# Block-diagonal attention matmuls in two row tiles of 64 partitions, with scores and values in two shared PSUM banks

## The reference, cut to what matters

```python
Q = (x @ Wq.T).reshape(b, length, 16, 16).swapaxes(-2, -1)     # x after a layer norm; K, V alike from the context
qk = jnp.einsum('blih,bljh->blij', Q, K) / sqrt(16)            # per token: a 16 x 16 matrix over its own features
attn = jax.nn.softmax(qk, axis=-1)
valued = jnp.einsum('blij,bljh->blih', attn, V)
x = x + tanh(g0) * (valued.swapaxes(-2, -1).reshape(b, length, d) @ Wo.T)
# then x + tanh(g1) * the output of the one expert with the largest gate, of the layer norm of x
```

## Time and profile before

| | us |
|---|---|
| median of three runs | 320.98 |
| the profiled execution, by its own time | 319.54 |
| span of that execution in the trace | 317.6 |
| TensorE matmuls busy | 285.0 (90%) |
| TensorE weight loads busy | 217.4 (68%) |
| VectorE busy | 230.9 (73%) |
| ScalarE busy | 84.4 (27%) |
| GpSimd busy | 123.2 (39%) |

### The profile page before, as it was taken

The page is one execution under the profiler, slowest core; times in us unless marked ns, Lnnn a source line. Parts: engine busy times, 40 slices in busy tenths (PEclk is TensorE's granted clock), DMA queues, the critical chain, the costliest instruction groups (busy, mean ns, idle before and its releaser), DMA issues.

```text
span 317.6 us, 10049 instructions
## 1 busy us (share of the span) xinstructions
PE 285.0 (90%) x3151; PEld 217.4 (68%) x3152; DVE 230.9 (73%) x810; ACT 84.4 (27%) x219; POOL 123.2 (39%) x125
## 2 busy tenths in 40 slices
PE   2999999999999999999999996687998899999970
PEld 1548677677677676776776775566877888898860
DVE  6576678797798888888877978855789556556550
ACT  1021321311312302303213213122434344444420
POOL 9321121523523523524424334432354444434441
PEclk9999999999999999999999999967999999999995
DMA  8565245475565575574455123166467878777620
GB/s 263 182 171 146 63 143 151 144 207 174 156 210 162 164 207 142 174 210 103 132 159 145 43 78 84 59 189 195 137 177 238 271 213 234 232 218 213 208 80 0
DMA packets 35482, 51.40 MB, mean 162 GB/s; under 512 B 8189, under 2 KB 18558, under 8 KB 35456
## 3 DMA queue, kind: packets, MB, share of 16 engines
q1 hardware_dynamic: 20272, 25.72, 31.2%
q10 hardware_dynamic: 11776, 16.78, 16.7%
q0 software_dynamic: 3408, 8.59, 7.4%
HBM read 32.99 MB, written 10.60 MB: 137 GB/s over the span
## 4 chain that ended last, share of the span: by engine, by line
PE 65%; DVE 13%; DMA 9%; issue 6%; ACT 2%; POOL 1%; ACTq 1%; SPq 1%; DVEq 1%; POOLq 0%
PE ps_qo L400 14%; PE ps_pr L392 13%; PE ps_tr L550 6%; DMA sb_x<-x_in 6%; PE ps_av L564 5%; PE ps_so L418 5%; PE ps_so L550 5%; PE ps_to L564 5%; PE ps_av L438 5%; PE ps_pr L540 2%; PE ps_tr L427 2%; DMA sb_wkv<-wkv_in 1%; PE ps_to L451 1%; DVE sb_om L787 1%; DVE sb_pe_x L763 1%
## 5 line engine op out<-in xcount | busy, mean ns | idle before, releaser
L392 PE MATMUL ps_pr<-sb_wkv,sb_ct 128*128 128x512 f32 x128 | 64.4, 628 | 6.4 <-DMA sb_wkv<-wkv_in 5.9
L278 POOL TENSOR_TENSOR sb_cn<-sb_om,sb_rt 128x512 f32<-128x512 f32 x15 | 19.3, 1285 | 67.6 <-DVE sb_om L787 67.6
L620 ACT ACTIVATE sb_pe_x<-sb_pe_x 128x512 f32<-128x512 f32 x16 | 10.1, 631 | 123.3 <-DVE sb_pe_x L763 123.3
L392 PEld LDWEIGHTS ps_pr<-sb_wkv,sb_ct 128*128 128x128 f32 x128 | 22.6, 194 | 25.8 <-issue 25.6
L1206 POOL DMA_INDIRECT routed_rows<-sb_xs,sb_pos_i x32 | 32.2, 1006 | 20.5 <-DVE sb_pos_i L878 10.5
L400 PE MATMUL ps_qo<-sb_wog,sb_ot 128*128 128x264 f32 x128 | 34.7, 419 | 1.3 <-ACT sb_q_n L615 1.1
L400 PEld LDWEIGHTS ps_qo<-sb_wog,sb_ot 128*128 128x128 f32 x128 | 26.1, 206 | 11.7 <-issue 7.3
L438 PE MATMUL ps_av<-sb_vb,sb_at 128*32 128x128 f32 x1024 | 31.6, 276 | 0.0
L418 PE MATMUL ps_so<-sb_kb,sb_y_q 128*32 128x128 f32 x1024 | 31.0, 273 | 0.3 <-DMA sb_kb<-sb_y_k 0.3
L400 PE MATMUL ps_qo<-sb_wqg_c,sb_xt 128*128 128x264 f32 x128 | 31.1, 387 | 0.0
L438 PEld LDWEIGHTS ps_av<-sb_vb,sb_at 128*32 128x32 f32 x1024 | 27.2, 111 | 5.6 <-issue 5.5
(11 more groups left out here) (127 smaller groups left out, 488.9 us busy)
## 6 DMA issues: line engine op xcount, KB each, us to landing
sb_w<-w_in_ SPq DMA_DIRECT2D x24, 257.0 KB, 3.1
sb_xb<-routed_rows SPq DMA_DIRECT2D x39, 134.0 KB, 2.5
sb_kb<-sb_y_k SPq DMA_DIRECT2D x125, 32.0 KB
sb_vb<-sb_y_v SPq DMA_DIRECT2D x124, 32.0 KB
sb_w<-w_in_ ACTq DMA_DIRECT2D x15, 257.0 KB, 3.4
sb_ct<-ctx_in ACTq DMA_DIRECT2D x15, 256.0 KB, 3.0
sb_x<-x_in ACTq DMA_DIRECT2D x15, 256.0 KB, 5.3
sb_xt<-xt_in_ ACTq DMA_DIRECT2D x14, 256.0 KB, 3.6
```

The source lines that it names most:

```text
L278: eng.tensor_tensor(cn[:].rearrange("p u h i -> p h u i"), om[:].rearrange("p h (u i) -> p h u i", u=2), rt[:].rearrange("p (u i) -> p u i ...
L392: last = pe.matmul(pr[:, s * 512:(s + 1) * 512], lhsT=ct[i][:, kc, s, :], rhs=wkv[:, kc, :], start=(kc == 0), stop=(kc == KC - 1))
L620: act.activation(pe_x[:], pe_x[:], ACT.Exp, scale=float(H) ** -0.5).then_inc(exp_done, 1)
```

## The change

The same products are formed, but each matmul has 64 partitions instead of 128 and 64 moving columns instead of 128; there are two of them where there was one: half g of the partitions with the four slots that are filled in it. They lie in two row tiles of TensorE's array. Per pair that is 64 matmuls each for scores and values, so 128 MATMUL and 128 LDWEIGHTS instructions each. Half g writes to bank g of a new tensor `sa` of two banks, in which values take columns 0 to 127 and scores columns 128 to 255 of each half bank.

As scores and values now lie in the same two banks, `turn_o(k-1)` on VectorE waits for the scores of k too (`score_done`, n + 2), and the read patterns of `largest`, `shift` and `turn_o` run over both banks. On TensorE the waits of values(k) and of scores(k+1) (K and V landed, `at_out`, `om_done`, `yq_out`, `sub_done`) are moved ahead of `project_o(k-1)`, and scores(k+1) are issued directly behind values(k) in the same slot. Ranks go to `to` instead of `av` (the last two to free parts of other banks), and `vb` keeps its slots in the order of `kb`.

```diff
-        so = ps("so", [P, 512])
-        av = ps("av", [P, 512])
+        sa = ps("sa", [P, 2 * 512])
+        sa_v = sa[:].rearrange("p (g a x) -> p g a x", g=2, a=2)
...
-            def scores(n, i):
-
+            def wait_scores(n, kb_landed):
+                pe.wait_ge(*kb_landed)
                 pe.wait_ge(yq_out, n + 1)
                 wait(pe, sub_done, n)
+
+            def scores(n, i):
                 for r in range(4):
                     for u in range(2):
                         for q in range(4):
                             b = 16 * u + 4 * q + r
-                            last = pe.matmul(so[32 * q:32 * q + 32, r * P:(r + 1) * P],
-                                             lhsT=y_q[:, 4 * q + r, u:u + 2, :].rearrange("p a b -> p (a b)"),
-                                             rhs=kb[i][:, :, H * b:H * b + H], start=(u == 0), stop=(u == 1))
+                            for g in range(2):
+                                half, own = slice(64 * g, 64 * g + 64), slice(4 * g, 4 * g + 4)
+                                last = pe.matmul(sa_v[32 * q:32 * q + 32, g, r // 2, P + 64 * (r % 2):P + 64 * (r % 2) + 64],
+                                                 lhsT=y_q[half, 4 * q + r, u:u + 2, :].rearrange("p a b -> p (a b)"),
+                                                 rhs=kb[i][half, own, H * b:H * b + H], start=(u == 0), stop=(u == 1))
...
             def slot(k, q, t):
-                pe.wait_ge(*landed(kb_in, q, t, 0, SPREAD))
-                scores(k, q)
...
                     project_kv(k + 2, q, 1)
+                if isinstance(k, int) and k == 0:
+                    wo_gates()
+                wait_values(k, landed(vb_in, q, t, 0, SPREAD))
+                if has(k, 1):
+                    wait_scores(k + 1, landed(kb_in, q, t, 1, SPREAD))
                 if has(k, -1):
                     project_o(k - 1)
-                if isinstance(k, int) and k == 0:
-                    wo_gates()
-                pe.wait_ge(*landed(vb_in, q, t, 0, SPREAD))
                 values(k, q)
+                if has(k, 1):
+                    scores(k + 1, 1 - q)
...
             def turn_o(n):
                 wait(dve, cn_done, n)
                 dve.wait_ge(av_done, n + 1)
-                dve.transpose(om[:], av[:].rearrange("p (t h) -> p h t", h=H)).then_inc(om_done, 1)
+                if not isinstance(n, int) or n < last_pair:
+                    dve.wait_ge(score_done, n + 2)
+                dve.transpose(om[:], sa_v[:, :, :, 0:P].rearrange("p g a (t h) -> p h t (g a)", h=H)).then_inc(om_done, 1)
```

More of the change, by code:

```diff
@@ L193, in flamingo_block @@
         x_t_ps = [pr[:, 512 * i:512 * i + D] for i in range(2)]
-        h_ps = [so[:, 0:D], tr[:, 0:D]]
-        y_ps = [av[:, 0:D], to[:, 0:D]]
+        h_ps = [tr[:, 0:D], sa[:, 0:D]]
+        y_ps = [sa[:, 512:512 + D], to[:, 0:D]]
         lap_ps = qo[:, 960:992]
         def rank_ps(n, first, end):
-            bank = qo[:, 448:512] if isinstance(n, int) and n == last_pair else av
+            bank = to
+            if isinstance(n, int) and n == last_pair - 1:
+                bank = sa[:, 512 + D:1024]
+            if isinstance(n, int) and n == last_pair:
+                bank = qo[:, 448:512]
             return bank[:, first:end]
@@ L428, in transpose_a, with wait_values, values @@
                 last.then_inc(at_done, 1)
-            def values(n, i):
+            def wait_values(n, vb_landed):
+                pe.wait_ge(*vb_landed)
                 pe.wait_ge(at_out, n + 1)
                 wait(pe, om_done, n)
-                wait(pe, rank_read, n - 1 if not isinstance(n, int) or n > 1 else 0)
+            def values(n, i):
                 for r in range(4):
@@ L437, in values @@
                             b = 16 * u + 4 * q + r
-                            last = pe.matmul(av[32 * q:32 * q + 32, r * P:(r + 1) * P],
-                                             lhsT=at[:, 4 * r + q, u:u + 2, :].rearrange("p a b -> p (a b)"),
-                                             rhs=vb[i][:, :, H * b:H * b + H], start=(u == 0), stop=(u == 1))
+                            for g in range(2):
+                                half, own = slice(64 * g, 64 * g + 64), slice(4 * g, 4 * g + 4)
+                                last = pe.matmul(sa_v[32 * q:32 * q + 32, g, :, 32 * r:32 * r + 32],
+                                                 lhsT=at[half, 4 * r + q, u:u + 2, :].rearrange("p a b -> p (a b)"),
+                                                 rhs=vb[i][half, own, H * b:H * b + H], start=(u == 0), stop=(u == 1))
                 last.then_inc(av_done, 1)
@@ L445, in transpose_o @@
                 wait(pe, ot_out, n)
+                if not isinstance(n, int) or n < last_pair:
+                    wait(pe, rank_read, n - 1 if not isinstance(n, int) or n > 1 else 0)
                 if isinstance(n, int) and n == 0:
@@ L467, in ranks @@
                 pe.wait_ge(oh_done, n + 1)
-                if not isinstance(n, int) or n < last_pair:
+                if isinstance(n, int) and n == last_pair - 1:
                     pe.wait_ge(om_done, n + 2)
+                elif not isinstance(n, int) or n < last_pair:
+                    pe.wait_ge(ot_out, n + 2)
                 rhs = oh_b[:].rearrange("p s e -> p (s e)")
@@ L528, in pre @@
                 pe.wait_ge(zero_ok, 1)
+                wait_scores(0, (kb_in[0], SPREAD))
+                scores(0, 0)
             slots(pe, pre, slot)
@@ L751, in scores_of, with by_half @@
             def scores_of():
-                return so[:].rearrange("p (t j) -> p t j", j=H)
+                return sa_v[:, :, :, P:2 * P].rearrange("p g a (r t j) -> p g a r t j", r=2, j=H)
+            def by_half(ap):
+                return ap[:].rearrange("p (g a r t) -> p g a r t", g=2, a=2, r=2)
             def largest(n):
                 dve.wait_ge(score_done, n + 1)
-                dve.tensor_reduce(mx[:], scores_of(), AX.X, ALU.max).then_inc(max_done, 1)
+                dve.tensor_reduce(by_half(mx), scores_of(), AX.X, ALU.max).then_inc(max_done, 1)
             def shift(n):
@@ L762, in shift @@
                 dve.wait_ge(max_done, n + 1)
-                dve.tensor_tensor(pe_x[:].rearrange("p (t j) -> p t j", j=H), scores_of(),
-                                  mx[:].unsqueeze(2).broadcast_to([P, 32, H]), ALU.subtract).then_inc(sub_done, 1)
+                dve.tensor_tensor(pe_x[:].rearrange("p (a r g t j) -> p g a r t j", a=2, r=2, g=2, j=H), scores_of(),
+                                  by_half(mx).unsqueeze(5).broadcast_to([P, 2, 2, 2, 4, H]), ALU.subtract).then_inc(sub_done, 1)
             def sums(n):
```

3 lines of the change are left out of this document (1 added, 2 removed).

## The result

The changed kernel takes 388.33 us (median of four runs, 385.97 to 393.69); the kernel before took 321.35 in the same comparison (319.21 to 322.07). The ratio is 1.211, with a 95% interval of 1.205 to 1.218: slower by a fifth. The forecast had the sign and the mechanism, but 337 us is far off and 388 lies above the range of 325 to 380.

What follows compares the result with a forecast made beforehand. TensorE bounds the attention stage, VectorE having only 2.1 us a slot to spare. New stalls make a slot 13.4 us instead of 12.16; 13 slots add 16 us to 319.5, then 1.4 to the median: 337 us, range 325 to 380.

Steps and rivals of the forecast that it cites:

- the constant 11.6: Attention slot's period outside the two matmul phases, in us: 9.57 to `turn_q`'s end, then 0.03, 1.87 and 0.15.
- P: Start-to-start cost of one values or scores matmul phase on TensorE; 1.78 us before the change.
- `turn_o`'s price of 0.71 us: VectorE's `turn_o` reading three strides over two banks: 0.71 us taken, other end +0.3 us a slot.
- The first stall: TensorE waits 1.75 us for the exponential at `transpose_a`; the output's transpose, ready at about +2.3, was taken as covered.
- P = 0.9: All eight tiles run side by side at the first bursts' pace, so each values or scores phase takes 0.9 us.
- R2: Rival: each matmul costs 27.8 ns whatever its columns; phase 3.56 us, slot 18.7 us, 406 us in all; chance 0.10.
- The cost of fetching, 0.3 us a slot: Allowance of 0.3 us a slot for fetching 256 more TensorE instructions per slot, within the range.
- The wait for the indirect DMA, 0.81 us: Wait in VectorE's chain before `turn_q`, taken to move along unchanged at 0.81 us a slot.
- R4: Rival: code fetching or a lower clock in the new stalls, the range's upper part; chance 0.04.
- R1: Rival: row tiles bring nothing; phase 1.78 us, slot 15.2 us, 360 us; chance 0.28 with what lies between.
- the main case: Full tile overlap, phases of 0.9 us, slot 13.4 us, 337 us in all; chance 0.45.
- R3: Rival: VectorE's chain is shorter and TensorE stays the bound; slot 10.4 us, 296 us; chance 0.13 with its neighbours.

Runs made afterwards that it cites:

- The order alone: Kernel before with its old matmuls and banks, but all waits and the scores' place as in the changed kernel: 385.15 us, ratio 1.207.
- the run with 64 columns alone: Kernel before with each scores and values matmul cut into two of 64 columns, all 128 partitions, old banks and order: 331.62 us, ratio 1.043.
- the run with the filler: Changed kernel plus four needless 128 by 264 matmuls in the stall ahead of the output projection: 385.85 us, ratio 1.214.
- The swap of `turn_q` and `place_4`: `turn_q` ahead of `place_4` in VectorE's list: changed kernel 360.28 us, ratio 1.132; kernel before 318.21 us, ratio 0.999.
- the last experiment: Changed kernel with lists reordered by readiness, ranks behind the second K and V projection and `turn_q` ahead of their reading: 348.11 us, ratio 1.090.
- The experiment before it: Changed kernel with lists reordered by readiness: waits back, `turn_q` first, statistics of k-2 ahead of `largest`, `turn_o` behind `shift`: 345.71 us, ratio 1.086.

## Why the prediction was wrong in size, and where it was right

**The bound (right).** TensorE and VectorE were both nearly full, and what VectorE does between the scores and `turn_q` decides. The waits that grew are in that chain; the holes of the first slots are not.

**The mechanism and the constant 11.6 (right, for undisturbed slots).** `turn_o` behind the scores, `transpose_a` late, the output projection behind `turn_q`: each is in the timeline above. The order alone measures 15.3 us a slot where 11.6 + 2P with the P of that kernel gives 15.1 to 15.2; in the changed kernel they take 15.05 where 11.6 and the 3.15 us of its phases make 14.75. `turn_o`'s price of 0.71 us was measured at 0.717. The first stall was split otherwise: a part of it, 0.34 us at 142.95, stands ahead of `transpose_o`, whose division was taken to be covered.

**P = 0.9 (failed).** The step that carried the pace of the first burst through the whole phase was wrong. In the slot shown, values and scores take 3.30 us in place of P + P + 0.15 = 1.95; before the change they took 129.29 - 125.58 = 3.71. So 0.41 us of the 1.76 expected came, about a quarter. The reading of the bursts as such was right, since 32 instructions start in the first 0.25 us, but the pace isn't kept. On four tiles 128 instructions need 1.99 us to their last result and on eight 1.48 at the best, and in the changed kernel's scores 1.9 to 2.0, no better than four. Why the pace falls is open. The Trainium skill speaks on both sides here as well. TensorEngine Tiling (Array Packing), Key Properties, has tiles load weights and multiply in parallel: the trace agrees that they do so in part. TensorE: Matmul & The Clock Gate, "Wait — 56ns, not 53.3ns?", has no two starts closer than about 25 ns: 128 instructions with their last result in 1.48 us are 11.6 ns each (23 ns for an fp32 matmul, which is two of them), so for these small tiles the trace does not agree, and R2 with it falls.

**The cost of fetching, 0.3 us a slot (failed).** The most of it is not spread over the slots. It comes in the first ones, as holes of up to 3.23 us, about 11 us together; the later slots of the run with 64 columns alone are 0.3 us over the mean before. That run has the holes too, without row tiles or a new order. That this is code being loaded is a reading of the instruction queue's packets, of their number and of their place beside the holes; no run held the number of instructions and changed only where the code lies.

**The wait for the indirect DMA, 0.81 us (failed).** It was carried along as a constant, from one row of a wait that nobody waited for. In all it was 10.6 us, 1.7 at the most; with the new order it is:

```profile
DVE sb_pos_i L902 <- DMA routed_rows<-sb_xs,sb_pos_i: 17.4, 11, 3.3
```

The cast's wait grew to 17.4 us, 3.3 at the most, and now all of it stands ahead of `turn_q`. When does it grow? In the longest case SyncE issues a late load of the expert weights 0.36 us behind the second scatter:

```profile
93.61 0.96 POOL L1230 DMA_INDIRECT routed_rows<-sb_xs,sb_pos_i  x1 [0.30 <-issue]
...
93.97 0.48 SPq L331 DMA_DIRECT2D sb_w<-w_in  x1
...
98.89 0.17 DVE L902 CAST sb_pos_i<-sb_pos 128x2 uint32<-128x2 f32 x1 [3.32 <-DMA routed_rows<-sb_xs,sb_pos_i]
```

In the traces of all these kernels every wait of the cast over 2 us, 14 in six kernels, stands where SyncE issues a load of expert weights or biases or a store of padding rows within 1 us of the second scatter; in the four steps of the changed kernel from 188.06 to 248.40, which have none of these DMAs, the cast waits 0.71 to 0.85 us, the 0.81 of the prediction. In the attention stage of the kernel before none of these DMAs comes so close to a second scatter. Not every close one is followed by a long wait, and no run moved these loads by themselves, so this is a strong coincidence and not a shown cause.

**The lower clock (R4, given 0.04 and no term in the sum; failed).** The output projection took 3.86, 3.67, 3.41 and 3.51 us in four steps instead of 2.02, which makes 6.4 us from start to start. In the run with the filler, which nearly kept the clock, longer waits for the DMA took its place.

**The sum.** The 14 steps took 234.21 us; the prediction makes 170.26 + 16 = 186.3 of them. Where the 47.9 us between them lie, read from the timeline:

| | us |
|---|---|
| 12 steps at 15.05 us undisturbed instead of 13.4 (16.2 of it is P, 1.35 each) | 19.8 |
| the first two steps, 34.3 instead of the 24.4 of before, with three of the five holes | 9.9 |
| two more holes | 4.5 |
| the cast's wait beyond 0.8 us, in seven steps | 8.7 |
| four output projections at the lower clock | 6.4 |

That is 49.3. The prediction's own sum has a slip that takes 1.2 off: of its 15 steps it leaves out three and then counts 13 in place of 12. The swap of `turn_q` and `place_4` takes the late DMAs off the path, and in the part shown no step is left at the lower clock.

**The rivals.** R1 (a slot of 15.2 us, 360 us) was near by its slot, 15.05 us undisturbed: in R1 values and scores take 3.71 us, in the main case 1.95, and 3.30 were measured. Holes, late DMAs and the lower clock did the rest. R2 falls with P. R3, the only way to a gain, is excluded: VectorE's chain kept its length, the cast's wait in it too. R4 was named as the range's upper part and was, with the late DMAs, most of what lies beyond R1; it should have had a size of its own.

**What the matmuls were worth by themselves.** Between the order alone and the changed kernel lie only the halved matmuls and the shared banks, and the ratios (1.207 and 1.211, with intervals that overlap) show no difference; the 14 steps take 234.44 and 234.21 us. That they agree so well is luck. Undisturbed slots get 0.2 to 0.3 us shorter (15.3 to 15.05), some 4 us in all, the holes at the start take 11, and the order alone happens to have more and longer steps with late DMAs and the lower clock. By the formula the change would have lost in this order even at P = 0.9.

## What to carry to other kernels

When two products come to share a bank, count the time of the reader of the first from the writer of the second, and follow that reader's engine to the end of its list; when a wait is moved ahead of independent work, that work's cover is lost for everything before the wait. A wait that stands in a profile beside slack has no fixed size: before it is put on the path, give it a range up to its longest value in the list of waits and more, since a new order also moves it against the other DMAs. A burst of a few instructions shows what pace is possible, not what is kept over a phase. Smaller matmuls on more tiles are worth trying only where the engine's time is set by columns and the program's code stays small; price twice the instructions in the first passes, not on the mean.

## What the runs showed of the hardware that was not expected

- fp32 matmuls of 64 partitions, 64 moving columns and 32 stationary columns on eight tiles: 128 MATMUL instructions with as many weight loads in 1.48 to 2.0 us to their last result, although 32 of them start in the first 0.25 us. On four tiles of 128 partitions the same number takes 1.99 us, about the same as 64 of 128 columns (1.95). The row tiles gave a quarter at the best, not a half.
- The scores phase was slower than the values phase in the changed kernel (1.92 against 1.51 us), and hardly so in the last experiment, where a wait and a semaphore stood between the two (1.55 and 1.49). The experiment before it has the same wait between them and scores phases of 1.7 to 1.9 us, so that isn't enough to explain it. Why is open.
- Doubling the instructions of two phases in each of 16 slots brought holes of up to 3.2 us in the first passes (5.4 from start to start in one kernel), with 0.09 MB more on the instruction queue.
- The wait for the same indirect DMA went from 0.6 to 3.5 us; all waits over 2 us stood beside another large DMA issued within 1 us of it.
- Stalls on TensorE were followed by matmuls at the lower of the two clocks, 1.2 GHz, in some slots and not in others, and the length of the stall doesn't tell which: in the changed kernel the output projection took 3.41 to 3.86 us behind stalls of 2.15, 2.45, 2.81 and 4.33 us, and 2.02 behind stalls of 2.26, 3.38 and 3.48. Two of these:

```profile
80.72 2.02 PE L403 MATMUL ps_qo<-sb_wog,sb_ot 128*128 128x264 f32 x8 [3.38 <-issue]
184.62 3.51 PE L403 MATMUL ps_qo<-sb_wog,sb_ot 128*128 128x264 f32 x8 [2.15 <-issue]
```
